# A transformer block with routed experts: shared weights parted beside attention, late down matrices, a reordered last step

## The reference

```python
h = tok(x, w_qkv, b_qkv, w_out, b_out)               # attention, (8, 512, 256)
h = concatenate([cls_tok, h], axis=1)                # 513 rows in a batch
h = h + ssm(layernorm(h), a_params, B_w, C_w, D)     # linear scan over the rows
h = h + ffn(layernorm(h), ...)                       # below

shared = silu(x @ Wg_s.T) * (x @ Wu_s.T) @ Wd_s.T
scores, idx = top_k(sigmoid(x @ Wr.T + rb), 2)
out = shared + sum over e of cw[e] * (silu(x @ Wg[e].T) * (x @ Wu[e].T) @ Wd[e].T)
```

## Time and profile before

| what | before |
|---|---|
| median of 3 runs | 1181.87 us (1180.08 to 1183.53) |
| the profiled execution | 1180.8 us, its span 1179.1 us |
| TensorE busy | 1118.6 us (95%) |
| VectorE busy | 913.3 us (77%) |
| ScalarE busy | 591.0 us (50%) |
| GpSimd busy | 399.1 us (34%) |
| mean granted TensorE clock | 0.983 |

### The profile page before, as it was taken

One profiled execution on the slowest core, in us unless ns is written; L12 is line 12 of the kernel. 1 busy time (PEld: TensorE's weight loads), 2 busy tenths in 40 slices (PEclk: granted clock), 3 DMA queues, 4 the chain that ended last, 5 costly groups with the idle time before them and its releaser, 6 DMA issues.

```text
span 1179.1 us, 22139 instructions
## 1 busy us (share of the span) xinstructions
PE 1118.6 (95%) x6022; PEld 714.0 (61%) x6023; DVE 913.3 (77%) x1567; ACT 591.0 (50%) x973; POOL 399.1 (34%) x516
## 2 busy tenths in 40 slices
PE   6998999999999999979999999977999999999996
PEld 3654233333333333467777877766888888888885
DVE  3788888888888888578887888877777777777775
ACT  3445777777777777641332222532444444444442
POOL 3011631101011010203455343462545555555553
PEclk9999999999999999989999999978999999999998
DMA  8786232323323232021444432311333333333332
GB/s 296 253 256 215 74 101 71 106 69 99 96 73 99 84 91 76 19 92 70 108 108 108 96 62 74 74 37 41 55 54 54 54 54 54 54 54 54 54 54 32
DMA packets 108691, 105.38 MB, mean 89 GB/s; under 512 B 42464, under 2 KB 97904, under 8 KB 108624
## 3 DMA queue, kind: packets, MB, share of 16 engines
q1 hardware_dynamic: 90528, 81.18, 24.2%
q0 software_dynamic: 18112, 23.57, 11.3%
HBM read 64.88 MB, written 39.68 MB: 89 GB/s over the span
## 4 chain that ended last, share of the span: by engine, by line
PE 72%; DVE 10%; issue 3%; POOL 3%; ACT 1%; DMA 0%; DVEq 0%; POOLq 0%
PE mix_pairs L73 19%; PE pv L673 10%; PE by_key L662 10%; PE by_query L653 9%; PE mix_made L1804 8%; PE mix_turn L1791 3%; PE mix_made L1244 2%; PE mix_made L1232 2%; POOL kept_table L1097 2%; PE mix_pairs L1270 2%; PE mix_turn L1771 1%; PE by_query L694 1%; PE mix_turn L1199 1%; PE mix_made L1215 1%; DVE mix_stats L1417 1%
## 5 line engine op out<-in xcount | busy, mean ns | idle before, releaser
L746 DVE TENSOR_REDUCE k_neg_max<-by_query 128x2 f32<-128x1024 f32 x240 | 282.4, 1219 | 54.2 <-PE by_query L653 53.5
L806 ACT ACTIVATE k_wu_e<-by_key 128x512 f32<-128x512 f32 x512 | 278.2, 600 | 82.3 <-PE by_key L662 78.9
L662 PE MATMUL by_key<-k_wg_e 99*128 99x512 bf16 x512 | 178.8, 382 | 3.2 <-DVE pv L782 3.0
L1747 POOL DMA_INDIRECT out_rows<-x_y,k_slot x72 | 114.0, 1583 | 159.4 <-PE mix_turn L1771 98.4
L653 PE MATMUL by_query<-k_wg_e 96*128 96x512 bf16 x480 | 143.4, 379 | 0.5 <-DVE k_neg_max L746 0.3
L1846 ACT ACTIVATE x_gate<-mix_pairs 128x512 f32<-128x512 f32 x72 | 43.0, 597 | 199.4 <-PE mix_pairs L73 199.4
L673 PE MATMUL pv<-k_wu_e,k_wd_e 128*17 128x512 f32 x1024 | 134.5, 598 | 0.3 <-ACT k_wu_e L806 0.3
L662 PEld LDWEIGHTS by_key<-k_wg_e 99*128 99x128 bf16 x512 | 42.0, 96 | 143.4 <-ACT k_wu_e L806 80.6
L73 PE MATMUL mix_pairs<-w_short,x_T 128*128 x288 | 121.6, 422 | 1.9 <-issue 1.9
L1804 PEld LDWEIGHTS mix_made<-x_wd,x_acts_T 128*128 128x128 f32 x864 | 111.2, 188 | 7.4 <-ACT x_acts_T L1868 0.9
L73 PE MATMUL mix_pairs<-w_short,x_rest 128*128 x288 | 114.6, 398 | 0.0
(11 more groups left out here) (242 smaller groups left out, 1951.6 us busy)
## 6 DMA issues: line engine op xcount, KB each, us to landing
k_wg_e<-kept_qk SPq DMA_DIRECT2D x384, 64.0 KB, 2.1
kept_qk<-k_qk_parts SPq DMA_DIRECT2D x32, 384.0 KB, 2.9
kept_v<-k_v_ones SPq DMA_DIRECT2D x8, 544.0 KB, 4.4
k_wd_e<-kept_v SPq DMA_DIRECT2D x32, 136.0 KB, 2.6
k_wu_e<-in_xT POOLq DMA_DIRECT2D x8, 512.0 KB, 5.6
kept_heads<-k_wd_e SPq DMA_DIRECT2D x8, 512.0 KB, 3.0
k_heads_in<-kept_heads SPq DMA_DIRECT2D x8, 512.0 KB
k_wg_e<-in_wg_e SPq DMA_DIRECT2D x8, 512.0 KB, 4.5
```

The source lines that it names most:

```text
L662: pe.matmul(by_key[:, key_bank(job), :], k_rows[0:SROWS, g, h, kt * P:(kt + 1) * P], q_rows[0:SROWS, g, h, :], start=True, stop=True).then ...
L746: dve.tensor_reduce(neg_max[:, g % 2, 2 * n:2 * n + 2], by_query[:, bank:bank + 2, :], AX.X, ALU.max, negate=True).then_inc(query_read, 1)
L806: act.activation(probs[:, key_tile(j) // 2 * G + j // 2 % G, j % 2, :], by_key[:, key_bank(job), :], ACT.Exp, scale=float(HD) ** -0.5).the ...
L1747: pool.indirect_dma_start(out=dram["out"], in_=y[:, r % 2, :], in_offset=None, compute_op=ALU.add, out_offset=bass.IndirectOffsetOnAxis(ap ...
```

## The change

- The shared expert's two matrices are parted in attention: ScalarE's copies in units 1 and 2 of batch 0, VectorE's subtractions in the work that it does beside attention (batch 0, unit 2, and the last batch, unit 0). Their remainder (w_s_rest) now lies in the place of the down matrices of experts 6 and 7, which SyncE loads behind the last gate product (`load_late`).
- `EARLY = 5`: numbers 0 to 4 are cut in steps 1 to 5, and the cut now stands behind `first_sum(b + 1)`. Numbers 5 and 6 are cut in step 7, and 7 to 15 in step 8.
- At the end of each step ScalarE copies u2_T first, out of PSUM, and makes u2_short from u2_T. `cut_second` subtracts from u2_T instead of the turned rows in PSUM. The router's product no longer waits for `u2_cut`.
- In step 7 `place` stands behind `normalise`. In step 8 TensorE makes two more half products ahead of `count`, cut 7 stands behind `count_tiles`, and the other cuts are spread anew.
- `list_adds` moves from step 8 to behind the first tile's activation. Two semaphores for lists become one, `lists_made`.
- Some buffers change places: u2_short and u2_rest lie where w_s_rest lay, heads_T and row_sum in u2.

```diff
@@ scalar(act, beside), attention
                 if j == 7 and not (isinstance(b, int) and b == 0 and g == 0):
-                    if isinstance(b, int) and (b, g) == (0, 1):
+                    copy_pv(*before(b, g))
+                    if isinstance(b, int) and (b, g) in ((0, 1), (0, 2)):
                         projections_stored()
-                    copy_pv(*before(b, g))
+                        beside(g - 1)
...
-EARLY = 3
+EARLY = 5
...
@@ SyncE
             def load_expert(e):
-                for name in ("wg_e", "wu_e", "wd_e"):
+                for name in ("wg_e", "wu_e", "wd_e") if e < E - 2 else ("wg_e", "wu_e"):
...
+            def load_late():
+                sp.wait_ge(ev["gate_made"], FC * B)
+                for e in (E - 2, E - 1):
+                    sp.dma_start(mem["wd_e"][:, bass.ds(e, 1), :, :], dram["wd_e"][:, bass.ds(e, 1), :, :]
+                                 ).then_inc(mem["experts_in"], 16)
...
                 if not this:
-                    sp.wait_ge(mem["tiles_listed"], 1)
+                    load_late()
+                    sp.wait_ge(mem["lists_made"], 1)
...
@@ ScalarE, step
                 if last:
-                    act.wait_ge(mem["experts_in"], 16 * 3 * (E - 2))
-                    shorten_weights(act, mem, 3)
+                    act.wait_ge(mem["experts_in"], 16 * (3 * (E - 3) - 2))
+                    shorten_weights(act, mem, 5)
                     act.wait_ge(ev["out_made"], 2 * B)
-                    shorten_weights(act, mem, 4)
+                    shorten_weights(act, mem, 6)
...
                 if this:
-                    copy_turned(short(u2_short), b, "u2_turned", "shared_shortened")
-
-                    act.wait_ge(ev["u2_cut"], b + 1)
                     copy_turned(u2_T, b, "u2_turned", "u2T_copied")
+                    act.wait_ge(ev["u2T_copied"], b + 1)
+                    act.activation(short(u2_short[:, :, :]), u2_T[:, :, :], ACT.Copy).then_inc(ev["shared_shortened"], 1)
...
@@ TensorE, step
                     if not this:
+                        shared_up(b - 1, 0, (1,))
+                        shared_up(b - 1, 1, (0,))
                         count(b - 1, nxt)
-                        shared_up(b - 1, 0, (1,))
-                    shared_up(b - 1, 1)
+                    shared_up(b - 1, 1, (0, 1) if this else (1,))
...
                     pe.wait_ge(ev["u2T_copied"], b + 1)
-                    pe.wait_ge(ev["u2_cut"], b + 1)
...
@@ VectorE
             def cut_second(b):
                 dve.wait_ge(ev["shared_shortened"], 2 + b + 1)
-                dve.tensor_tensor(short(u2_rest[:, :, :]), turn[:, :, :], u2_short[:, :, :],
+                dve.tensor_tensor(short(u2_rest[:, :, :]), u2_T[:, :, :], u2_short[:, :, :],
                                   ALU.subtract).then_inc(ev["u2_cut"], 1)
...
                         count_tiles(dve, cls_link, mem, flat_backs)
+                        cut_weights(dve, mem, 7)
                     shared_act(b - 1, 1)
                     if not this:
                         list_tiles(dve, cls_link, mem, flat_backs)
-                        list_adds(dve, cls_link, mem, flat_backs)
-                if 1 <= b <= EARLY:
-                    cut_weights(dve, mem, b - 1)
...
                     if not this:
-                        for n in (5, 6, 7, 8):
+                        for n in (8, 9, 10):
                             cut_weights(dve, mem, n)
...
                 if not prev:
                     class_act()
-                elif this:
+                elif nxt:
                     place(b - 1, 1 - par)
                 if this:
                     dve.wait_ge(ev["u2_turned"], b)
                     dve.wait_ge(ev["u2_stored"], 16 * b)
                     normalise(b, h2[:, par, :, :], 2)
+                if this and not nxt:
+                    place(b - 1, 1 - par)
                 if prev:
                     shared_add(b - 1, 1 - par, 0)
                     if not this:
-                        for n in (9, 10, 11):
+                        for n in (11, 12, 13):
                             cut_weights(dve, mem, n)
                     shared_add(b - 1, 1 - par, 1)
                     if not this:
-                        for n in range(12, 2 * E):
+                        for n in range(14, 2 * E):
                             cut_weights(dve, mem, n)
                 if this:
                     cut_second(b)
                 if nxt:
                     first_sum(b + 1)
-                if not prev:
-                    dve.wait_ge(ev["cls_up"], 1)
-                    for n in range(2):
-                        dve.wait_ge(ev["shared_shortened"], n + 1)
-                        dve.tensor_tensor(short(w_s_rest[:, n, :, :]), w_s[n][:, :, :], w_s_short[:, n, :, :],
-                                          ALU.subtract).then_inc(ev["w_s_cut"], 1)
+                if 1 <= b <= EARLY:
+                    cut_weights(dve, mem, b - 1)
                 if not prev:
                     class_add()
                 if this and not nxt:
-                    for n in (3, 4):
+                    for n in (5, 6):
                         cut_weights(dve, mem, n)
...
             def beside(g, n):
...
                     class_statistics(0)
+                    cut_shared(0)
                 elif (g, n) == (B - 1, 0):
                     class_norm(0, cls_u, "cls_u")
+                    cut_shared(1)
...
@@ VectorE, experts
         cut_down(0, 0)
         act(0, 0)
+        list_counts()
         body(0, False)
```

More of the change, by code:

```diff
@@ L1641, in _ @@
             batches(dve, step)
-            experts[4](dve)
+            experts[4](dve, lambda: list_adds(dve, cls_link, mem, flat_backs))
 def count_tiles(dve, link, mem, scratch):
@@ L2062, in program @@
                 with ExitStack() as alias:
-                    mem["w_s_rest"] = alias.enter_context(nc.sbuf_tensor("w_s_rest", [P, 2, DC, F], FP32))
+                    for part in ("u2_short", "u2_rest"):
+                        mem[part] = alias.enter_context(nc.sbuf_tensor(part, [P, TT, D], FP32))
             if name not in mem:
```

60 lines of the change are left out of this document (35 added, 25 removed).

## The result

The changed kernel takes 1193.42 us (median of four runs, 1191.58 to 1194.50), the kernel before, run beside it, 1181.64: a ratio of 1.0097, 95% interval 1.0078 to 1.0117. It is slower, as forecast, but by 11.8 us and not 5.9, and the time lies 0.4 us above the range. The profiled executions are 1191.5 and 1179.1 us long, 12.4 apart.

The account below looks back on a forecast made before the run. TensorE was taken to wait for VectorE at two seams, and on a closed chain of engines in each 34.94 us step. 6.4 + 4.4 - 2.6 + 2.5 + 1.0 - 5.8 = +5.9 on 1181.87 gave 1187.8 us, range 1180.0 to 1193.0.

Parts of the forecast that it names:

- Part 1: End of steps 1 to 6: ScalarE's new order puts 1.07 us more in front of cut_second and the first sum, +6.4.
- Part 2: Steps 1 to 5: a cut behind first_sum makes GpSimd's power end 0.89 us later, +4.4.
- The rival in which the power gets in first: Steps 1 to 5: GpSimd's power starts before the cut, the clock holds, 1180.9 us, no change; chance 0.20.
- Part 3: Steps 0 and 1: first scan ends earlier, -1.4, and the clock's fall at L1244 is avoided, -1.2.
- Part 4: Steps 1 to 5: TensorE's pause before the turn grows to 2.5 us; two clock falls of five, +2.5.
- The row that was to show 1.70 as safe: Pause of 1.70 us in front of L1330: window still shows 0.96, taken as nearly all at 2.4 GHz.
- Part 5: Attention: two ScalarE copies and two VectorE subtractions move in, +1.0, between 0 and 2.6.
- The sign of being wrong, TensorE below 97% busy: Attention: TensorE below 97% busy would show the attention term wrong.
- Part 6: Last batch step and start of the experts: first row copy comes earlier, together -5.8, bounds -6.9 and -4.0.
- its last term: First tile: rows must be gathered behind the table writes, so the copy starts at about 805.3, -6.3 instead of -6.9.
- The one with the clock falling in all five steps: Steps 1 to 5: clock term is 6.2, sum +9.6, 1191.5 us; chance 0.15.
- The side that said faster, with TensorE setting the step: Batch steps: TensorE, not the chain, sets the step; order, cuts and clock cost nothing, -7.4, 1174.5 us; chance 0.08.

Follow-up runs that it names:

- run 1: Changed kernel with ScalarE's old order back (u2_short first, VectorE subtracting from PSUM, router product waiting for u2_cut): 1185.16 us, 1.0043 to the kernel before.
- run 2: Changed kernel with the five early cuts back in the middle of the step, ScalarE's new order kept: 1191.37 us, 1.0098 to the kernel before.
- run 3: Changed kernel with both ScalarE's old order and the early cuts in the middle of the step: 1182.65 us, 1.0009 to the kernel before.
- run 7: Kernel before with only its three early cuts moved behind the first sum: 1181.10 us, 1.0002 to the kernel before.
- run 10: run 6 with the first early cut (batch 1) moved behind shared_add, in front of cut_second: 1173.75 us, 0.9953 to the kernel before.
- run 9: Changed kernel with TensorE repeating the first three shared-expert products twice in batches 1 to 6, results overwritten: 1189.23 us, 1.0086 to the kernel before.
- run 4: Changed kernel with ScalarE's copies and VectorE's subtractions of the shared matrices moved between attention and step 0: 1192.34 us, 1.0099 to the kernel before.
- run 8: Changed kernel with only VectorE's two shared subtractions moved between attention and step 0, ScalarE's copies still in attention: 1192.18 us, 1.0100 to the kernel before.
- run 5: Changed kernel with ScalarE's old order in batches 0 to 6 and the new one in batch 7 alone: 1182.31 us, 1.0016 to the kernel before.
- run 6: Changed kernel with shared parting between attention and step 0, early cuts mid-step, ScalarE's new order in batch 7 alone: 1175.67 us, 0.9961 to the kernel before.

## Why the prediction was right in its direction and short in its size

- **Part 1, the order: right.** 1.07 a period was foreseen, 1.08 to 1.10 measured (runs 1 to 3). Its sign was misnamed: 2.1 us from the turn of u2 to `cut_second` was already the distance before (664.90 to 667.03). Now it is 3.2, and 2.14 is counted from the copy.
- **Part 2, the power behind the cut: right.** 0.89 foreseen, 0.89 to 0.91 measured, and run 7 shows it without the rest. The rival in which the power gets in first has no case in any trace: every power behind a cut took 1.93 or 1.94.
- **Part 3, steps 0 and 1: right in sum.** With a period's +1.07 and +0.89 it gives -0.64 from the end of attention to step 2's turn, which is what the landmarks show (2.93 - 3.57). The split was otherwise: step 0 gained 1.4 and not 0.7, step 1 lost 0.8. The pause in front of L1244's products was 1.88 us and the sixteen took 3.92, so the clock held in this execution. It did not in run 10, after the same pause, nor in three more of the six traces with such a pause, so that these -1.2 came true is partly luck.
- **Part 4, the clock: the step that failed by most.** The forecast took "two falls of five" at 1.24. There were three, all behind pauses of 2.8 us (counted at 2.5), and a fourth at the turn of step 7, behind a pause of 1.9 (counted at 1.6 and as safe). Each cost 1.4 to 1.6, not 1.24, since it slows more products than L1244's sixteen: about 6.0 us in place of 2.5. Run 9 shows that the pauses are the cause. The row that was to show 1.70 as safe was misread. Its window ends at 524.00, and the clock fell at 523.84 by the trace's clock record, 1.5 us behind the start of the router's product, which is why it shows 0.96 and not 1.00. The six microseconds behind it are at 1.2 GHz throughout (columns as in the earlier trace rows):

```profile
524.00:530.00 6.00, 3.17 (x9) 2.57 (x9) 5.62 (x21) 1.26 (x2) 1.93 (x1) 0.50 0.24 77
```

In the table pauses of 1.87 to 1.96 lost the clock in 6 cases of 9, and no case up to 1.46 did.
- **Part 5, attention: the step whose mechanism failed.** It was put at +1.0 with an upper bound of 2.6, "both subtractions in full and a little for ScalarE". The four insertions cost 3.3 us (run 4), half of it by ScalarE (run 8), and the fall of the clock at its start, which no term had, another 0.9; attention began 0.6 earlier. ScalarE at 76% had idle time because it waited for TensorE: in the kernel before, 78.9 of the 82.3 us in front of its exponentials (L806) end with `by_key`. It was no reserve, and the bound charged it almost nothing. VectorE's idle pieces were the wrong thing to look at: its subtractions cost 1.7 us because GpSimd was held beside them, which is part 2's own mechanism. The sign of being wrong, TensorE below 97% busy, could not have shown it: it is 98.8% busy from 120 to 500 us after, 99.2% before, and 1% of that window is 3.8 us.
- **Part 6, the last step and the first tile: near in size, partly by luck.** -5.8 foreseen, -5.6 measured, with the gather as the new limit, as its last term said. Up to the first product of the tiles it is -4.9 for -6.3, and the tiles then took 0.7 less, not 0.5 more. The kernel of run 7, the same as before in this stretch, took 2.4 us less than the one before, so about that much of the -4.9 can be the clock's. The table writes, put at 0.5 us for what falls into cuts, took 2.0 us longer. What it missed too is that the new order earns 2.4 to 3 of this, by the earlier router product; it called that product's earlier start worth nothing in a steady step, which is true, and gave its 2.3 us in step 7 back almost whole.
- **The sum.** 6.4 + 4.4 - 2.6 + 6.0 + 3.6 - 5.6 = 12.2 with the two terms replaced (attention is 4.2 less the 0.6 by which it started early), against 12.4 between the spans. The range was missed, by 0.4 us, because its upper end, 1193.0, was five falls at 1.24 with attention at its bound of 2.6: the falls came to as much (6.0 for 6.2), and attention to 1.0 more than its bound.
- **The rivals.** The one with the clock falling in all five steps came nearest in time, 1191.5, but with four falls at 1.5 in place of five at 1.24, and with attention at 1.0. The side that said faster, with TensorE setting the step, has no support: the period followed the chain in every run to a tenth of a microsecond.

## What to carry to other kernels

An engine that feeds a TensorE without idle time may have no spare time even at 76% busy: here a copy of 1.05 us on it cost 0.8. Look for a buffer that is ready ahead by as much as the insertion takes. A VectorE subtraction with both inputs in SBUF is to be placed by what GpSimd has to do beside it, not by VectorE's idle time: it cost 0.9 us a step and 0.8 us in attention, each time through GpSimd. A reordering that pays once, at the last pass, can cost its price in every pass; where the loop is unrolled, do it in the last pass alone (runs 5 and 6). Of a pause that grows in front of TensorE count the clock as well as the pause, and where work can't be moved into it, a few repeated products can hold the clock, as in run 9, whose gain in the time stayed within the noise.

## What the runs showed of the hardware

- At the turns the clock fell behind 6 of 9 pauses of 1.9 us and 10 of 15 of 2.8. In the changed kernel and run 8 it fell at the turns of steps 2, 3, 5 and 7, in run 4 at that of step 6 too, with the same pauses. Why one falls and its neighbour doesn't stays open; such kernels are best compared by their undisturbed periods.
- GpSimd's casts and sums of 128x16 in attention are held by a VectorE subtraction with both inputs in SBUF: 1.26 us for 0.20 and 1.07 for 0.21 (the changed kernel against runs 8 and 4).
- GpSimd's table writes are held too. In the changed kernel:

```profile
716.39 1.23 DVE L1440 TENSOR_TENSOR u_rest<-k_mix_u_T,u_short 128x1024 fp32r<-128x1024 f32 x1 [2.20 <-ACT u_short L1180]
...
716.45 2.01 POOL L1104 DMA_INDIRECT kept_table<-k_pay,k_slot_i  x1 [0.30 <-issue]
```

The write is begun 0.06 us behind a subtraction of 1.23 with both inputs in SBUF, and takes 2.01 us in place of 0.98, ending 0.84 behind it, like the power (569.06). Before, this subtraction read the turned rows in PSUM. The mean of the 64 writes rose from 1019 to 1130 ns, 7 us in all, of which 3 to 4 go with the new order (1080 in run 1, 1063 against 1129 in runs 3 and 2). In the steps they are hidden; in step 8 they are not, for the gather follows them. The Trainium skill's page "SBUF — State Buffer", section "Who interferes with whom", infers that such a subtraction leaves descriptor generation alone. This row shows that an indirect write, at least, is held. Whether its descriptors wait or its read of the slots in SBUF was not separated.
- A scan waits as well: 2.46 us for 1.28 when it meets GpSimd's sum of two tensors (run 10), with an end 1.09 us behind the sum's.
